# Lane marks numbered by ScalarE and GpSimd, products and zeroing moved at two seams, and fourteen unread products, in a fused attention and expert kernel

## What is computed

```python
q, k, v = Wq@xf + bq, Wk@xf + bk, Wv@xf + bv          # MID = 32 for q and k
x = alpha * (v @ softmax(q.T @ k).T) + x              # per image, 1024 x 1024
t = tokens(x)                                         # 4 x 1024 tokens of 256
z = ln(t); prods = proxy @ z.T                        # 16 proxies
w = softmax(prods / 4, over the proxies)
t = t + sum_p w[p, s] * cumsum_s(prods[p, s] * z[s])  # causal, by state and mask
z = ln(t); logits = z @ gate_w.T                      # 8 experts, the best two
t = t + sum of the two: share * (gelu(z @ w1[e] + b1[e]) @ w2[e] + b2[e])
```

## Time and profile before

| | us |
|---|---|
| median of 3 runs | 832.53 (831.14 to 834.49) |
| the profiled execution: time | 832.61 |
| the profiled execution: span | 830.9 |
| busy: TensorE matmul / weight load | 721.0 / 682.9 |
| busy: VectorE, ScalarE, GpSimd | 503.1, 310.9, 399.7 |
| mean granted clock of TensorE | 0.941 of 2.4 GHz |

### The profile page before, as it was taken

How to read it: one execution, slowest core, us unless ns; L and a number is a source line. 1 busy time by engine, 2 the same in 40 slices (tenths; PEclk the granted TensorE clock), 3 DMA queues, 4 the chain that set the end, 5 groups by cost and what they waited for, 6 DMA issues and landing times.

```text
span 830.9 us, 18535 instructions
## 1 busy us (share of the span) xinstructions
PE 721.0 (87%) x5410; PEld 682.9 (82%) x5411; DVE 503.1 (61%) x1152; ACT 310.9 (37%) x599; POOL 399.7 (48%) x462
## 2 busy tenths in 40 slices
PE   5898998989558667634999999999999999999993
PEld 4797897978546555424999999999999999999993
DVE  3787787877665989972545544554455445544551
ACT  2664854736324434212323332333223322332230
POOL 1564563734944323225355555555555555555233
PEclk9999999999968989855999999999999999999997
DMA  7569476493351212122175653754565445544222
GB/s 263 197 224 416 155 275 246 174 399 140 148 225 56 97 59 102 53 78 60 27 249 154 179 193 62 239 158 141 179 209 157 140 145 152 146 140 145 27 27 28
DMA packets 45868, 130.08 MB, mean 157 GB/s; under 512 B 5184, under 2 KB 35520, under 8 KB 41216
## 3 DMA queue, kind: packets, MB, share of 16 engines
q1 hardware_dynamic: 30560, 104.86, 33.4%
q0 software_dynamic: 13904, 19.45, 13.5%
q10 hardware_dynamic: 1360, 5.24, 1.6%
HBM read 186.80 MB, written 47.59 MB: 282 GB/s over the span
## 4 chain that ended last, share of the span: by engine, by line
PE 51%; issue 1%; DMA 1%; POOL 1%; DVE 0%; POOLq 0%; ACT 0%; DVEq 0%
PE ps_h L73 9%; PE ps_h L74 8%; PE ps_h L75 8%; PE ps_y L73 8%; PE ps_y L75 8%; PE ps_y L74 8%; PE ps_x L1545 2%; DMA out_tok<-y,to_row 0%; POOL out_tok L1425 0%; DMA x_rows<-normed,from_row 0%; POOLq L1348 0%; DVE yb L1505 0%; DVE xtl L1485 0%; DVE y L1512 0%; ACT xth L1450 0%
## 5 line engine op out<-in xcount | busy, mean ns | idle before, releaser
L1459 ACT ACTIVATE g<-ps_h,bias 128x256 f32<-128x256 f32 x288 | 120.8, 471 | 278.8 <-PE ps_h L75 278.8
L1425 POOL DMA_INDIRECT out_tok<-y,to_row x72 | 118.5, 1645 | 160.4 <-DVE y L1512 148.6
L73 PE MATMUL ps_h<-xth,wbuf 128*128 128x256 f32 x576 | 164.3, 285 | 3.3 <-issue 1.8
L73 PE MATMUL ps_y<-wbuf,gl 128*128 x576 | 164.5, 286 | 0.0
L74 PE MATMUL ps_h<-xtl,wbuf 128*128 128x256 f32 x576 | 164.1, 285 | 0.0
L75 PE MATMUL ps_h<-xth,wbuf 128*128 128x256 f32 x576 | 162.8, 283 | 0.0
L75 PE MATMUL ps_y<-wbuf,gh 128*128 x576 | 161.5, 280 | 0.0
L74 PE MATMUL ps_y<-wbuf,gh 128*128 x576 | 161.5, 280 | 0.0
L73 PEld LDWEIGHTS ps_h<-xth,wbuf 128*128 128x128 f32 x576 | 109.2, 190 | 3.9 <-issue 2.1
L75 PEld LDWEIGHTS ps_h<-xth,wbuf 128*128 128x128 f32 x576 | 110.8, 192 | 0.0
L74 PEld LDWEIGHTS ps_h<-xtl,wbuf 128*128 128x128 f32 x576 | 109.5, 190 | 0.0
(11 more groups left out here) (235 smaller groups left out, 1369.5 us busy)
## 6 DMA issues: line engine op xcount, KB each, us to landing
wbuf<-wsplit SPq DMA_DIRECT2D x71, 2048.0 KB, 7.3
wsplit<-wbuf SPq DMA_DIRECT2D x14, 2048.0 KB, 12.0
wraw<-in_w SPq DMA_DIRECT2D x16, 1024.0 KB, 7.6
raw<-in_x_ch ACTq DMA_DIRECT2D x5, 1024.0 KB, 10.1
normed<-x SPq DMA_DIRECT2D x8, 528.0 KB, 3.1
tok<-in_x_tok SPq DMA_DIRECT2D x1, 4096.0 KB, 16.6
out_tok<-tok SPq DMA_DIRECT2D x8, 512.0 KB, 3.7
x_rows<-normed,from_row POOLq DMA_INDIRECT x72, 3.2
```

The lines of the kernel that those rows point to most:

```text
L73: eng.matmul(out, ll, rh, start=first, stop=False)
L1425: pool.indirect_dma_start(out=out, out_offset=bass.IndirectOffsetOnAxis(ap=to_row[:, par, s:s + 1], axis=0), in_=y[:, par, s, :], in_offse ...
L1459: last = act.activation(g[:, f, :], ps_h[:, q, f % 2, :], ACT.Gelu_apprx_tanh, bias=bias1[:, bass.ds(e, 1), f:f + 1].rearrange("p a f -> p ...
```

## The change

1. `BATCHES` has four entries, of 16, 8, 4 and 4 tiles. The first is done at the end of the third image (now also written out), the second and third within the last image, the fourth where the third was. The steps on VectorE and ScalarE move with it.
2. At the start of stage B the zeroing is done buffer by buffer, `prepare` raises a new semaphore `turn_in` after two copies, and TensorE's `turn` waits for that alone; ScalarE evacuates chunk 0's transposes ahead of its first normalisation; the zeroing of `ps_rec` comes one round later.
3. In `mark_cells` VectorE writes one lane mark per pair, ahead of the cell marks, with one operation. ScalarE multiplies all of them by the partition's number, GpSimd by the tile's.
4. The matmul of the counts goes ahead of the last record.
5. Stage C opens on TensorE with fourteen matmuls of the identity by itself, into a bank that nobody reads.

```diff
-BATCHES = ((0, NT - IT), (NT - IT, NT - REST), (NT - REST, NT))
+BATCHES = ((0, NT - 2 * IT), (NT - 2 * IT, NT - IT), (NT - IT, NT - REST), (NT - REST, NT))
+LAST = len(BATCHES) - 1
...
-            with eng.Fori(0, B - 1) as b:
+            with eng.Fori(0, B - 2) as b:
                 image(b, True)
+            image(B - 2, True)
             image(B - 1, False)
...
                                            wbuf[:, par, at:at + n].bitcast(F32), ALU.subtract).then_inc(w_lo, 1)
+                        if more and isinstance(b, int) and (par, part) == (0, 1):
+                            tok.products(pool, fixed, *BATCHES[0], 0)
                         if not more and par == 0:
-                            tok.products(pool, fixed, *BATCHES[part], part)
+                            tok.products(pool, fixed, *BATCHES[1 + part], 1 + part)
...
-                    if it < B - 1:
-                        tok.mean_var(dve, it * IT, (it + 1) * IT, 0, it == B - 2)
-                    if it == REST:
+                    if more and it < 2:
+                        tok.mean_var(dve, it * IT, (it + 1) * IT, 0, it == 1)
+                    if more and it == IT - 2:
+                        tok.softmax_in(dve, *BATCHES[0], 0)
+                    if not more and it == 0:
                         tok.mean_var(dve, *BATCHES[1], 1)
-                        tok.softmax_in(dve, *BATCHES[0], 0)
-                    if it == IT - 2:
                         tok.softmax_out(dve, *BATCHES[0], 0)
+                    if not more and it == REST - 1:
                         tok.softmax_in(dve, *BATCHES[1], 1)
-                    if it == IT - 1:
+                    if not more and it == REST:
+                        tok.mean_var(dve, *BATCHES[2], 2)
+                    if not more and it == REST + 1:
                         tok.softmax_out(dve, *BATCHES[1], 1)
+                    if not more and it == IT - 2:
+                        tok.softmax_in(dve, *BATCHES[2], 2)
+                    if not more and it == IT - 1:
+                        tok.softmax_out(dve, *BATCHES[2], 2)
...
-            def next_tile(c):
-                wait_apart(pool, lane_d, done(c))
+            def lanes_by_tile(c, par):
+
+                pool.wait_ge(lane_d, done(c))
+                pool.wait_ge(rec_mm, done(c - 2))
+                pool.tensor_tensor(lane_tile[:, par].rearrange("p (k b) l -> p k b l", k=2),
+                                   lane[:, :, :].rearrange("p (k b) l -> p k b l", k=2),
+                                   tile_no[:, :].unsqueeze(1).unsqueeze(3).to_broadcast([P, 2, B, P]), ALU.mult).then_inc(lane_tile_d, 1)
+                wait_apart(pool, lane_tile_d, done(c))
                 pool.tensor_scalar(tile_no[:, :], tile_no[:, :], 1.0, None, ALU.add).then_inc(tile_d, 1)
+                wait_apart(pool, tile_d, done(c))
...
             pool.wait_ge(const0, 1)
-            pool.wait_ge(zeroed, 1)
             body(-2, 0)
+            pool.wait_ge(zeroed, 3)
             pool.memset(causal[:, :], 1.0).then_inc(const0, 1)
...
+            def lanes_by_part(c, par):
+
+                act.wait_ge(lane_d, done(c))
+                act.wait_ge(rec_mm, done(c - 2))
+                act.activation(lane_part[:, par], lane[:, :, :], ACT.Copy, scale=part_id[:, 0:1]).then_inc(lane_part_d, 1)
...
                 dve.wait_ge(spot_d, done(c))
+                dve.wait_ge(lane_tile_d, done(c - 1))
+                dve.wait_ge(lane_part_d, done(c - 1))
+                for kb in range(KB):
+                    last = dve.tensor_scalar(lane[:, kb, :], lane_id[:, :], spot[:, 0, kb:kb + 1], None, ALU.is_equal)
+                last.then_inc(lane_d, 1)
                 dve.wait_ge(rec_mm, done(c - 2))
                 for kb in range(KB):
                     last = dve.tensor_scalar(cell[:, par, kb, :], column_id[:, :], spot[:, 1, kb:kb + 1], None, ALU.is_equal)
                 last.then_inc(cell_d, 1)
-                wait_apart(dve, tile_d, done(c - 1))
-                for k in range(2):
-                    for b in range(B):
-                        mine = spot[:, 0, k * B + b:k * B + b + 1]
-                        dve.tensor_scalar(lane_tile[:, par, k * B + b, :], lane_id[:, :], mine, tile_no[:, b:b + 1],
-                                          ALU.is_equal, ALU.mult)
-                        last = dve.tensor_scalar(lane_part[:, par, k * B + b, :], lane_id[:, :], mine, part_id[:, 0:1],
-                                                 ALU.is_equal, ALU.mult)
-                last.then_inc(lane_d, 1)
...
-            dve.memset(prod[:, :, :], 0.0)
-            dve.memset(weight_t[:, :, :, :], 0.0).then_inc(zeroed, 1)
+            dve.memset(prod[:, 0], 0.0).then_inc(zeroed, 1)
+            dve.memset(weight_t[:, 0], 0.0).then_inc(zeroed, 1)
+            dve.memset(prod[:, 1], 0.0)
+            dve.memset(weight_t[:, 1], 0.0)
...
             def turn(c):
-                pe.wait_ge(prep_d, done(c))
+                pe.wait_ge(turn_in, done(c))
...
+                if isinstance(i, int) and i == CH + 1:
+                    pe.wait_ge(count_d, done(CH - 1))
+                    pe.wait_ge(attn_d, done(CH - 1))
+                    pe.matmul(ps_count, ones[:, :], counts_m[:, :], start=True, stop=True).then_inc(counted, 1)
                 if exists(i - 2):
                     record(i - 2, par)
...
+            def unread():
+
+                for _ in range(14):
+                    pe.matmul(ps_y[0][:, 0, 0:P], ident[:, :], ident[:, :], start=True, stop=True)
...
+                if lo == 0:
+                    unread()
                 turn_x(lo, lo % SLOT)
```

More of the change, by code:

```diff
@@ L428, in image @@
                         exp_tile(it + 2)
-                    if not more and it in (REST + 1, IT - 2):
-                        n = it // (IT - 2)
+                    if not more and it in (REST, IT - 2):
+                        n = 1 + it // (IT - 2)
                         tok.exponential(act, *BATCHES[n], n)
@@ L441, in image @@
                     whole_qk(b + 1, 1)
+                if isinstance(b, int) and b == B - 2:
+                    tok.exponential(act, *BATCHES[0], 0)
             load_x(0)
@@ L558, in image @@
                         statistics(g)
-                    if not more:
+                    if isinstance(b, int):
                         routing_weights(it)
@@ L746, in stage_b @@
             "newly count hot_rank place_f place_i spot_i spot")
-        lane_d, tile_d, cell_d = sems("lane tile_no cell")
+        lane_d, lane_tile_d, lane_part_d, tile_d, cell_d = sems("lane lane_tile lane_part tile_no cell")
         x2_d, tok_out = sems("x2 tok_out")
@@ L808, in prepare @@
                 if isinstance(c, int):
-                    pool.wait_ge(tok.weights_d, 2 if c < REST else 3)
+                    pool.wait_ge(tok.weights_d, LAST if c < REST else LAST + 1)
                 else:
-                    pool.wait_ge(tok.weights_d, 3)
+                    pool.wait_ge(tok.weights_d, LAST + 1)
                 prods = chunk_of(tok.t[:, :, :], c)[:, :, C:C + NP]
                 pool.tensor_copy(prod_in[:, :, 0:NP], prods)
-                pool.tensor_copy(weight_in[:, :, 0:NP], chunk_of(tok.weights[:, :, :], c))
+                pool.tensor_copy(weight_in[:, :, 0:NP], chunk_of(tok.weights[:, :, :], c)).then_inc(turn_in, 1)
+                if isinstance(c, int) and c == 0:
+                    pool.wait_ge(zeroed, 1)
                 pool.tensor_copy(prod[:, par].rearrange("p (b n) -> p b n", b=B)[:, :, 0:NP], prods)
@@ L896, in _ @@
             pool.wait_ge(routing_set, 2)
-            tok.products(pool, fixed, *BATCHES[2], 2)
+            tok.products(pool, fixed, *BATCHES[LAST], LAST)
             for i in range(-1, 2):
@@ L903, in _ @@
         def _(act):
-            for s in (turned_d, x1_d, gexp_d, x2_d):
+            for s in (turned_d, x1_d, gexp_d, x2_d, lane_part_d):
                 act.sem_inc(s, CREDIT)
@@ L1207, in attend @@
                 pe.wait_ge(state_d, done(c - 1))
+                pe.wait_ge(prep_d, done(c))
                 for b in range(B):
@@ L1238, in record @@
             def record(c, par):
-                pe.wait_ge(lane_d, done(c))
+                pe.wait_ge(lane_tile_d, done(c))
+                pe.wait_ge(lane_part_d, done(c))
                 pe.wait_ge(cell_d, done(c))
@@ L1259, in body @@
                     turn(i + 2)
-            pe.wait_ge(zeroed, 2)
-            pe.matmul(ps_rec[:, :], nothing[:, 0:P], nothing[:, :], start=True, stop=False)
             for i in range(-2, 2):
+                if i == -1:
+                    pe.wait_ge(zeroed, 3)
+                    pe.matmul(ps_rec[:, :], nothing[:, 0:P], nothing[:, :], start=True, stop=False)
                 if i == 1:
@@ L1267, in _ @@
             middle_and_end(pe, body)
-            pe.wait_ge(count_d, done(CH - 1))
-            pe.wait_ge(attn_d, done(CH - 1))
```

(1 more changed line is left out.)

24 lines of the change are left out of this document (14 added, 10 removed).

## The result

The changed kernel takes 822.36 us (median of 4 runs, 822.08 to 827.73) against 833.18 for the kernel before (831.14 to 834.49): ratio 0.9893, 95% interval 0.9872 to 0.9914. Forecast were 816.5 us and a range of 804 to 823.5. The median itself lies just inside that range; against the 832.53 us that the forecast started from, the ratio of 0.9893 is 823.6 us, just outside. One of the four executions took 827.73, so the ratio says 8.9 us of gain and the medians 10.8. The profiled execution took 822.62 us, around a span of 820.9; the span of before was 830.9, so the two traces differ by 10.0 us.

A forecast was written before the change was run, and what follows sets the result against it. From 397 us TensorE is fully busy on untouched matmuls, so only time ahead counts. Terms 7.9 + 1.0 + 0 + 3.7 + 3.0 = 15.6, said as 16.1 with some of 0.7: 816.5 us, range 804 to 823.5.

The forecast's parts named there:

- Seam (a): Last attention image, TensorE's 10.37 us wait for ScalarE's weight load: new batches gain 7.9 us, ends 6 and 9.5.
- VectorE's L148 for the third batch has two SBUF inputs and falls into the second: Last attention image: L148 waits for GpSimd's second L359 until 229.1, needs 2.5 us more, ends at 231.6.
- Its products for 4 tiles wait for the statistics of 215.81 + 0.37 = 216.2: Last attention image: GpSimd's third-batch products start at 216.2, run to 219.8; two L359 end at 224.4 and 229.0.
- the price in the image ahead: Image before the last: earlier products delay L488 by 1.2 us, new softmax start adds 0.8; 1.8 us taken as loss.
- Into routing: Seam from attention into routing: ScalarE starts 3 us earlier, 1.0 us gained; 0, or 1.5 lost if met at 1.2 GHz.
- The rounds: Routing rounds: VectorE saves 2.2 us each but waits for GpSimd; 0 us per round, 0.7 over all with a shorter product.
- the port: Routing rounds: cell marks share VectorE's port with GpSimd's product; six wait to m+8.0 (m: mask), record starts m+9.4.
- Rival 1: Warm rounds: TensorE stays at 2.4 GHz through routing records, round 12.1 us, total 807 us; chance 0.29, whole or part.
- rival 2: Routing rounds: cell marks do not share the port with GpSimd; round 10.9 us, total 800 us; chance 0.09.
- The table: End of routing: with the count matmul earlier, the table runs beside the last record; 3.7 us gained.
- Fourteen products: Opening of the expert part: unread matmuls keep layer one fast, 2.5 us, plus 0.5 in four transposes; 3.0 us gained.
- 0 if the clock falls again in the two short waits: Opening of the expert part: lower bound of the 3.0 us term, no gain if TensorE's clock falls up to 386.

The follow-up runs named there:

- e1: Changed kernel with two softmax ends of the last attention image moved by one tile (16 tiles: later, 8 tiles: earlier); 817.85 us.
- e2: Changed kernel with both lane products of the routing rounds on ScalarE, none on GpSimd; 821.23 us.
- e3: Changed kernel without its fourteen unread matmuls at the opening of the expert part; 829.17 us.
- e5: Changed kernel with the lane marks of the kernel before: VectorE makes all sixteen with two operations each; 829.98 us.
- e7: Changed kernel with the count matmul behind the last record again; 827.52 us.
- e8: Changed kernel with the edits of e1 and e2 and eight more unread matmuls in the second pair's wait of the expert part; 809.38 us.
- e9: e8 with the seam into routing as in the kernel before and six unread matmuls in the first pair's wait; 809.08 us.
- e10: e9 with the lane products split: VectorE makes those of two of the four tile numbers, ScalarE the rest; 806.68 us.
- e6: Changed kernel with the front of routing as before: whole zeroing first, transposes behind all preparation, ScalarE in its old order; 821.98 us.
- e12: Kernel before, with only VectorE's small scale product written as TENSOR_SCALAR with alpha as the scalar; 832.49 us, ratio 1.0001.
- e4: Changed kernel with the attention batches of the kernel before (24, 4 and 4 tiles), softmax and products called where they were; 825.29 us.
- e11: e10 with VectorE's small scale product in the attention part written as TENSOR_SCALAR with alpha as the scalar; 804.66 us.

## Why the prediction was wrong

*Seam (a), 7.9 us: the failed step.* GpSimd's own lengths held: products for 8 and 16 tiles took 4.8 and 6.9 us (said 4.7 and 7.0). The step "VectorE's L148 for the third batch has two SBUF inputs and falls into the second" looked at one such instruction and left out the others that the new batches place: L164 for 16 and for 8 tiles, both with two SBUF tensors, and the L558 behind them. I had the mechanism and the earlier trace rows, and laid out only the last batch against the L361.

In the prediction's terms, what broke is "Its products for 4 tiles wait for the statistics of 215.81 + 0.37 = 216.2": that time was taken from the old trace, plus a price of 1.8, so 218.0. L164 for 16 tiles now stands ahead of these statistics on VectorE and waits for an L361; they came 5.2 us later than that, the products at 223.19, and the two L361 ended at 235.66 and not at 229.0 + 1.8 = 230.8. In e1, without this wait, the chain is the forecast's: products at 218.32, L361 end at 230.82, part end at 234.1 for 233.4.

By e1 the two calls cost 5.2 us, and by means too: the part ended at 241.1 in six executions with them (the changed kernel, e2, e3 and e5 to e7) and at 235.8 in e1, e8, e9 and e10. Of the forecast gain 7.2 us are there without them in e1, and 5.5 by that mean. The rest is the price in the image ahead, 2.5 for 1.8: L494 (L488 of before) ended 1.8 us later, where 1.2 was counted. The wait of ScalarE for its load, with the 10.37 us of TensorE behind it, is gone from this trace, as worked out.

The rule of the Trainium skill (SBUF — State Buffer, Who interferes with whom) is that an operation of VectorE with two inputs in SBUF contends with a GpSimd instruction that reads SBUF, and one with a single input, outside certain modes, does not. L164 at 3.12 us beside an L361, L558 at 2.97 with two tensors and 0.20 with one, and L511, which has one of its inputs in PSUM and took 1.20 us beside an L361, agree. The 0.42 us of L164 in e1 does not fit as simply: it ran beside a GpSimd instruction that also reads SBUF (L126 on 128x8 elements, from 204.29 for 1.65 us) and was not held. What held VectorE for long here were GpSimd's products of 1024 and 2048 elements.

*Into routing, +1.0.* Wrong sign in seven traces of eight, by 1.9 between the changed kernel and e6. The start did come sooner (the first mask 9.6 us behind the part's end, before 11.6: 2.0 us, not 3), but the lower bound in the prediction ("a loss of 1.5 if TensorE meets that at 1.2 GHz") is what took place: the products of output(0), two records each, follow each other after 0.88 us (253.07, 253.95 in the timeline) up to 256.5, and after 0.44 behind it. In e1, where they met 2.4 GHz, the new order did win 0.9 us. I should have asked what TensorE does in the gap that an earlier start opens.

*The rounds, 0.* The weakest step by the forecast's own word, the port, was right, and so was the product (1.95 us mean, said 2.1). What was missed is smaller: the record stands at m+9.0 and not m+9.4, as GpSimd's product runs m+5.7 to m+7.8 and not m+5.9 to m+8.0. The 3.1 us are 1.25 in the first two rounds from the third mask (27.75 and now 26.50), 0.17 in each of the next three, and 1.3 behind the last mask, where TensorE's waits ahead of the last three records are 0.46, 0.43 and 0.34 us shorter. The term was put at 0 and measured 3. Rival 1's round came once in five and did not make this gain. The prediction's "third rival" beside the port's rule is its rival 2.

*The table, 3.7*: 3.9 in the traces, 3.7 by e7, as worked out.

*Fourteen products, 3.0.* In the first pair they gave that: from 383.49 to 396.90 it was 13.4 us, and now from 375.41 to 385.78 10.4. The step "0 if the clock falls again in the two short waits" left out the second pair, which ran at 2.4 GHz before; here it fell, 1.5 us. The change need not be the cause: the second pair also fell in e3 and in e12, without the fourteen products. In e1, e4, e6 and e7, with the fourteen products alone, the opening took 17.7 us each time, as in the changed kernel; in e2 and e5 the first pair fell as well (19.2 and 19.1), so the fourteen did not protect it every time.

So the sum of 15.6 became 9.6: 5.9 lost at seam (a), 1.7 in front of routing, 1.5 in the opening, 3.1 won in the rounds.

## What to carry to other kernels

Where VectorE and GpSimd share a port, list every VectorE operation with two SBUF inputs that an edit moves, also a tiny one, and lay each against GpSimd's long products; a 0.15 us operation can cost 3, and moving it by one tile cost nothing here, giving it one tensor operand 0.05 us. When a step of one engine is laid out anew, take the times of all that hangs on it from the new order too: the statistics that failed the forecast were read from the old one. A shorter wait or an earlier start is worth its time only if TensorE does not meet the next work at the lower clock, so read the granted clock of every stretch behind the edit. Removing such a stall pays only when it is what ends last: the same line gave 2 us in the median in one kernel and nothing measurable in the other.

## What the runs showed of the hardware

The same attention code, in one execution each of the changed kernel, e2, e3, e5, e6 and e7, ended at 239.3, 244.8, 243.3, 240.3, 239.1 and 239.7 us. In the two late ones ScalarE waits 2.1 us for a load of weights, which it doesn't in the changed kernel and e5, and the last image of e2 started 0.6 us sooner than the changed kernel's, so all of the delay comes within that image. What decides between the outcomes was not found; one profile shows one of them. This is why stretches are compared above. Single-input operations of VectorE on float32 (L160, L162, L554, L558 as TENSOR_SCALAR on one element) ran beside an L361 in 0.14 to 0.39 us, whereas the CAST waited; eight 16-bit TENSOR_SCALAR of 256 elements took 3.35 us beside a 2.05 us product and 1.65 without it.

The idle time ahead of a record of routing does not by itself tell its clock. In the changed kernel, e1 and e7 the one record behind 3.17 to 3.20 us ran at 2.4 GHz to its end and those behind 3.29 or more did not, but the last record of each, behind 2.8 us, did not either, and e10 and e11 break the order altogether: behind the same 3.34 us the first record of e10 ran at 2.4 GHz throughout (1.91 us, granted clock 1.00) and that of e11 mostly at 1.2 GHz (3.52 us, 0.53), and behind only 1.84 us the last record of e10 ran at 1.2 GHz (3.57 us, 0.50).

```profile
275.01:276.92 1.91, 1.91 (x17) 1.74 (x18) 1.91 (x5) 0.27 (x2) 1.06 (x6) 1.00 0.00 0
348.98:352.55 3.57, 3.57 (x16) 2.17 (x16) 3.19 (x12) 0.00 (x0) 0.00 (x0) 0.50 0.02 5
```

The two rows are the stretches of these records of e10.
